# A two-layer attention and expert kernel: layer one's weighted values, one block of 32 products in every unit, become one block of 64 in every second unit

## The chip, the cores and the metric

The kernel runs on one core of a Trainium2 chip, all of it in one launch. The metric is the device time of that launch in microseconds; a lower one is better. TensorE (PE) multiplies, VectorE (DVE), ScalarE (ACT) and GpSimd (POOL) do the element-wise work, SyncE (SP) issues most DMAs. Each engine works through its own list of instructions in order and waits on semaphores that others raise.

## What is computed

Input: x (64 batches, 128 rows, 128 features), a side input of the same shape and a context of 120 rows per batch. In short:

```python
x = x + L0_xattn(layernorm(x), side, ctx, ctx)   # 16 heads of 8; keys: 128 projected + 120 given
x = x + L0_ffn(layernorm(x))                     # top 2 of 8 experts, silu(a) * g
x = x + L1_xattn(layernorm(x), ctx, ctx)         # 16 heads of 8; 120 keys
x = x + L1_ffn(layernorm(x))                     # top 2 of 8 adapters, gelu
# an attention, per batch and head:
attn = softmax(q @ k.T * scale); out = attn @ v
```

The change lies in the first line, the attention over 248 keys.

## The kernel before

`encoder` (L2066) runs five phases one behind the other: constants, layer one's attention (`attention_layer`, L103, with `first` true), the expert tiles, layer two's attention, the adapters. The 64 batches are 16 groups of four. A **step** g of the attention (L97) has eight **units** u; a unit is one batch and eight of its 16 heads. Step g scores group g, takes the row maxima of group g+1 and prepares g+2 and g+3. So steps 0 to 14 hold scores and maxima, step -1 maxima alone and step 15 scores alone.

Five engines walk the same list `UNIT` (L145). Its entries: **scores** i (L1033) is four bf16 products of 122 rows by 128 columns into one of three PSUM banks, i even for the 128 projected keys, i odd for the 120 others; ACT turns each into weights (`exponent`, L719, instruction L725) in `p_t`. **max** i (L1048) is two bf16 products of 248 columns into one of two banks (NMX = 2), and DVE reduces each to two columns of maxima (`row_maxima`, L873, instruction L876). **job** i is projections, transposes and router work at fixed places (table at L133); PE fills a misc bank (L978), ACT or DVE empties it. **values** i (L1066) is half of a unit's weighted values: with the two passes of an f32 product 16 of the 32 products of L1086, which work in four strips of PSUM `ps_o` side by side. It works on the unit before (`prev_unit`, L289), whose weights are complete by then.

What sets the order: PE, DVE and ACT each follow `UNIT` entry by entry; DVE and ACT have nothing at a values entry. DVE adds side work behind each maximum (`between`, L918: input statistics and the router's stages, table at L1445) and empties the jobs VP, OB and OP before the next maximum.

The waits that matter: PE's maximum tile n waits until DVE has read tile n-2 (L1059), its scores tile n until ACT has read n-3 (L1040). A values block waits for the weights of its unit (L1077), and in the first and fifth unit for ACT's copy of `ps_o` (L1080). ACT's weights buffers are two, so the first exponent of unit u waits until the values of unit u-2 are done (L724).

```python
wait(pe, max_read, i - NMX + 1)                                    # L1059
pe.wait_ge(sc_read, sc_no(g, u, (quarter + 1) * NT))               # L1077
wait(pv_done, g.n * UPS + u - 1)                                   # L724, on ACT, for i == 0
```

Of the kernel before, what the change touches and what calls it, by code (L numbers as in the profile page):

```python
# [81 lines left out]
def wait(eng, sem, value):  # L82

    if isinstance(value, int) and value <= 0:
        return
    eng.wait_ge(sem, value)
# [16 lines left out]
def attention_layer(nc, x_in, x_out, side_t_in, ctx_in, ctx_t_in, layer, consts, route, stacks, second, expert_w=None,  # L103
# [12 lines left out]
    first = layer == 0  # L116
# [26 lines left out]

    if first:
        UNIT = [  # L145
            ("job", 0), ("scores", 0), ("max", 0), ("scores", 1), ("job", 1), ("max", 1), ("values", 0),
            ("values", 1), ("scores", 2), ("max", 2), ("scores", 3), ("job", 2), ("max", 3),]
    else:
        UNIT = [
            ("job", 0), ("scores", 0), ("max", 0), ("scores", 1), ("values", 0), ("values", 1), ("job", 1),  # L150
            ("max", 1),]
# [5 lines left out]

    def stored_in(b):
        return -3 if b < 4 else -2

    def job_group(u, place, name, b):
        if name in ("SK", "SV"):
            return b - stored_in(b)
        if name == "XT" and not first:
            return 3
        if name == "KP" and not first:
            return 3
        if name in ("XT", "QP", "KP"):
            return 2
        if name == "VP":  # L170
            return 1 if first else 0
        if name == "RC":
            return -2
        if name in HEAD_JOBS:
            return 0
        if name in ("AT", "OP", "RX", "RQ"):
            return -1
        if name == "OB":
            return -1 if u < 3 else 0
        return 1 if u >= 2 else 0  # L180
    def head_step(name, b):
        return Group(0, 0) + (NG if (name, b) == ("FG", 1) else NG - 1)
    def job_runs(g, job):
        if job[2] in HEAD_JOBS:
            return g.n == head_step(*job[2:]).n
        if job[2] in ("SK", "SV"):
            return g.n == stored_in(job[3])
        if not first and job[2] in ("KP", "VP") and 0 < (g + job_group(*job)).n + (job[2] == "VP") <= STORED - (job[2] == "KP"):
            return False
        return (g + job_group(*job)).exists  # L190
# [21 lines left out]
    with ExitStack() as c:  # L212
# [76 lines left out]
        def prev_unit(g, u):  # L289
            return (g, u - 1) if u else (g + -1, UPS - 1)  # L290

        def jobs_at(g, u, place, engines_jobs=None):
            return [(k, j) for k, j in enumerate(jobs) if j[:2] == (u, place) and job_runs(g, j)
                    and (engines_jobs is None or j[2] in engines_jobs)]
# [4 lines left out]
        def stored_values(g):  # L299
            return not first and 0 <= g.n < STORED  # L300

        def emptied(eng, gj, name, b=0):

            n = job_done(gj, name, b) - 1
            if n >= 0:
                eng.wait_ge(misc_emptied[n % 2], n // 2 + 1)
# [668 lines left out]
        def _(pe):  # L975
# [57 lines left out]
            def scores(g, u, i):  # L1033

                b, hf, p = u // 2, u % 2, g.par
                t, quarter = CHUNKS[i]
                n = sc_no(g, u, i)
                if i == 0 and hf == 0 and b % 2 == 0:
                    pe.wait_ge(shift_loaded[p][b // 2], (g.pair + 1) * 32)
                wait(pe, sc_read, n - NSC + 1)  # L1040
                k0 = sum(KEYS[:t])
                for j in range(4):
                    h = hf * HALF + quarter * 4 + j
                    last = mm(ps_sc[n % NSC][0:KEYS[t], j * S:(j + 1) * S], k_st[p][:, b // 2, h, b % 2, k0:k0 + KEYS[t]],  # L1044
                              q_st[p][:, b // 2, h, b % 2], start=True, stop=True)
                last.then_inc(sc_filled, 1)

            def max_tile(g, b, k):  # L1048

                p = g.par  # L1050
                i = mx_no(g, b, k)
                if first and g.n == 0 and b == 0:
                    if k == 0:
                        pe.wait_ge(first_half_loaded, 16 * 2 * NPART)
                    elif k == MT_PER_B // 2:
                        pe.wait_ge(st_loaded[0][0], 16 * 2 * NPART)
                elif k == 0 and b % 2 == 0:
                    pe.wait_ge(st_loaded[p][b // 2], (g.pair + 1) * 16 * 2 * NPART)
                wait(pe, max_read, i - NMX + 1)  # L1059
                for j in range(HPB):  # L1060
                    h = k * HPB + j
                    last = mm(ps_mx[i % NMX][:, j * NK:(j + 1) * NK], q_st[p][0:TERM_TOP, b // 2, h, b % 2],  # L1062
                              k_st[p][0:TERM_TOP, b // 2, h, b % 2], start=True, stop=True)
                last.then_inc(max_filled, 1)

            def weighted_values(g, u, quarter):  # L1066

                b, hf, p = u // 2, u % 2, g.par
                if u == 0 and quarter == 0:

                    if stored_values(g):
                        pe.wait_ge(v_formed, g.n + 1)
                    else:
                        emptied(pe, g, "VP")
                    if first:
                        pe.wait_ge(v_ctx_ready, g.n + 1)
                pe.wait_ge(sc_read, sc_no(g, u, (quarter + 1) * NT))  # L1077
                if u % 4 == 0 and quarter == 0:

                    pe.wait_ge(o_read, g.n * 2 + b // 2 + 1)  # L1080
                for t in range(NT):
                    for strip in range(4):
                        j = quarter * 4 + strip
                        r, col = 32 * strip, ((b % 2) * 2 + hf) * S
                        at = (hf * 4 + strip) * V_PAIR + quarter * 2 * (DH + 1)
                        last = mm(ps_o[r:r + 2 * (DH + 1), col:col + S], v_t[t][p][:, b, at:at + 2 * (DH + 1)],  # L1086
                                  p_t[t][u % 2][:, j * S:(j + 1) * S], start=(t == 0 and quarter == 0),
                                  stop=(t == NT - 1 and quarter == 1))
                if quarter == 1:
                    last.then_inc(pv_done, 1)  # L1090

            def step(g):
                g1 = g + 1
                for u in range(UPS):
                    gp, up = prev_unit(g, u)
                    for what, i in UNIT:
                        if what == "job":
                            for k, j in jobs_at(g, u, i):
                                fill(g, k, j)
                        elif what == "scores" and g.exists:  # L1100
                            scores(g, u, i)
                        elif what == "max" and g1.exists:
                            max_tile(g1, u // 2, (u % 2) * MT_PER_U + i)
                        elif what == "values" and gp.exists:
                            weighted_values(gp, up, i)
            if first:
                pe.wait_ge(route.consts_loaded, 48)
            run_steps(pe, step, LAST_STEP)


# [955 lines left out]
def encoder(nc, a, out):  # L2066

    x3 = nc.dram_tensor("x3", (NG, S, GB, D), F32, kind="Internal").ap()
    xs = nc.dram_tensor("routed_in", (ROUTED_ROWS, ROW), F32, kind="Internal").ap()
    ys = nc.dram_tensor("routed_out", (TOKENS * TOP + 2 * E * S, D), F32, kind="Internal").ap()  # L2070
    x1, second = (ys[0:TOKENS * TOP].rearrange("(g k s b) d -> k g s b d", k=TOP, s=S, b=GB)[k] for k in range(TOP))
    with ExitStack() as c:
        route, stacks = Route(nc, c, xs), Stacks(nc, c)
        consts = constants(nc, c, a["w_attn"], a["b_attn"], a["b_rows"], a["wqkv_t"], route)
        attention_layer(nc, a["x"], x1, a["side_t"], a["ctx"], a["ctx_t"], 0, consts[0], route, stacks, second,
                        expert_w=(a["w1_t"], a["w2_t"]))
        expert_tiles(nc, ys, route, stacks)
        head = AdapterHead(nc, c, route, x3, a["wg_t"], a["bg"], a["W1_t"], a["W2_t"])
        attention_layer(nc, x1, x3, None, None, a["ctx_t"], 1, consts[1], route, stacks, second, head=head)
        adapter_layer(nc, x3, out, head)  # L2080
# [46 lines left out]
```

## Time and profile before

| | us |
|---|---|
| median of three runs | 1431.8 (1426.97 to 1435.11) |
| the profiled execution | 1426.79, its span 1424.7 |
| PE busy over the span | 1271.9 (89%) |
| DVE busy | 1072.4 (75%) |
| ACT busy | 838.4 (59%) |
| POOL busy | 882.7 (62%) |
| mean granted clock of TensorE | 0.952 |

Busy time of PE is the time in which at least one matmul is in the array; matmuls overlap, so an always busy PE can still have waits between them. The start-to-start distance in the timeline tells more. Layer one's blocks of values run from 72 to about 575 us of the span.

### The profile page before, as it was taken

Reading aid. Unit: us, or ns where it says so; the run is one execution under the profiler, and the core shown is the slowest. Engines: PE = TensorE matmul, PEld = TensorE weight load, DVE = VectorE, ACT = ScalarE, POOL = GpSimd, SP = SyncE. Lnnn points to the kernel's source line nnn. Section 1 sums busy time; section 2 is a strip of 40 time slices with the busy share of each in tenths; the row PEclk is TensorE's granted clock in tenths of the full one; section 3 lists DMA queues with packets and bytes.
Section 4 is the critical chain, followed back from the end, with each engine's and each line's share of the span. In section 5 each row is a group of like instructions: output and inputs, shape, how many; then the busy total and the mean of one; then the engine's idle time right before and its main releaser. Section 6 shows DMA issues by size and latency. Waiting matters only on the chain. (4 is left out here: it accounts for less than half of the span.)

```text
span 1424.7 us, 44434 instructions
## 1 busy us (share of the span) xinstructions
PE 1271.9 (89%) x16309; PEld 1054.9 (74%) x16309; DVE 1072.4 (75%) x3393; ACT 838.4 (59%) x1590; POOL 882.7 (62%) x949
## 2 busy tenths in 40 slices
PE   2689999999999999379999999668999999968998
PEld 0377787787777787279999999536777788746776
DVE  4678999989989996547766666457888888835774
ACT  3167777777777767156666666235666666634552
POOL 6346888888878856547777777534554444125660
PEclk9799999999999999689999999779999999968999
DMA  6776677777777760535555555487888888534784
GB/s 185 218 218 205 220 248 245 238 242 241 239 230 233 223 189 31 192 56 64 66 65 66 64 65 64 95 235 222 259 266 268 259 263 243 158 80 115 185 186 139
DMA packets 212638, 252.15 MB, mean 177 GB/s; under 512 B 38328, under 2 KB 173752, under 8 KB 205400
## 3 DMA queue, kind: packets, MB, share of 16 engines
q1 hardware_dynamic: 179768, 226.33, 52.7%
q0 software_dynamic: 25840, 21.71, 10.9%
q8 instruction: 131, 2.15, 0.6%
q10 hardware_dynamic: 6816, 1.29, 0.5%
q14 instruction: 83, 0.68, 0.2%
HBM read 156.73 MB, written 91.46 MB: 174 GB/s over the span
## 5 line engine op out<-in xcount | busy, mean ns | idle before, releaser
L876 DVE TENSOR_REDUCE L_neg_max<-L_ps_mx 128x2 f32<-128x496 f32 (+1 forms) x768 | 489.4, 661 | 100.9 <-PE L_ps_mx L1062 98.5
L725 ACT ACTIVATE L_p<-L_ps_sc 120x512 f32<-120x512 f32 (+1 forms) x768 | 417.5, 598 | 207.3 <-PE L_ps_sc L1044 203.7
L1062 PE MATMUL L_ps_mx<-stack_k,stack_q 118*128 118x248 bf16 (+1 forms) x2048 | 299.1, 250 | 42.7 <-DMA stack_q<-L_q_rows 26.1
L1044 PE MATMUL L_ps_sc<-stack_q,stack_k 122*120 122x128 bf16 (+1 forms) x3072 | 300.2, 221 | 3.7 <-ACT L_p L725 2.5
L1044 PEld LDWEIGHTS L_ps_sc<-stack_q,stack_k 122*120 122x120 bf16 (+1 forms) x3072 | 239.5, 123 | 56.8 <-issue 35.4
L1563 POOL DMA_INDIRECT routed_out<-M_y,M_x x135 | 212.0, 1570 | 87.8 <-DVE M_y L1654 86.8
L1086 PE MATMUL L_ps_o<-L_p,L_v 120*18 120x128 f32 (+1 forms) x6144 | 220.8, 276 | 2.5 <-ACT L_o_sb L754 2.1
L1062 PEld LDWEIGHTS L_ps_mx<-stack_k,stack_q 118*128 118x128 bf16 x2048 | 141.7, 100 | 103.4 <-issue 35.1
L1086 PEld LDWEIGHTS L_ps_o<-L_p,L_v 120*18 120x18 f32 (+1 forms) x6144 | 147.7, 98 | 37.7 <-issue 24.7
L1433 POOL DMA_INDIRECT routed_in<-R_xn,R_slot x128 | 127.0, 993 | 42.2 <-issue 36.2
L1609 ACT COPY M_w<-stack_k 128x768 f32 x135 | 112.1, 832 | 53.6 <-PE M_ps_g L1586 36.3
L1586 PE MATMUL M_ps_a<-M_xT,M_w 128*128 128x128 f32 x810 | 113.4, 276 | 0.0
L1586 PE MATMUL M_ps_g<-M_xT,M_w 128*128 128x128 f32 x810 | 113.2, 276 | 0.0
L1595 PE MATMUL M_ps_y<-M_w,M_hT 128*128 128x128 f32 x810 | 112.6, 275 | 0.0
L522 POOL TENSOR_TENSOR L_rem<-L_qf,L_q_parts_sb 128x512 f32<-128x512 f32 x30 | 34.8, 1161 | 122.0 <-ACT L_q_parts_sb L663 122.0
L1614 ACT ACTIVATE M_act_a<-M_ps_a 128x384 f32<-128x384 f32 x135 | 66.3, 491 | 73.0 <-PE M_ps_a L1586 72.4
L1586 PEld LDWEIGHTS M_ps_a<-M_xT,M_w 128*128 128x128 f32 x810 | 102.0, 193 | 0.1
L1586 PEld LDWEIGHTS M_ps_g<-M_xT,M_w 128*128 128x128 f32 x810 | 101.9, 193 | 0.0
L1595 PEld LDWEIGHTS M_ps_y<-M_w,M_hT 128*128 128x128 f32 x810 | 101.3, 192 | 0.2 <-DVE M_hT L1646 0.2
L1635 DVE COPY M_w<-stack_q 128x384 f32 x135 | 49.1, 364 | 63.4 <-issue 61.0
L1646 DVE TENSOR_TENSOR M_hT<-M_act_a,M_ps_g 128x384 f32<-128x384 f32 x135 | 74.8, 554 | 26.8 <-ACT M_act_a L1614 22.6
L522 POOL TENSOR_TENSOR L_rem<-L_kf,L_k_parts_sb 128x512 f32<-128x512 f32 (+1 forms) x23 | 27.8, 1209 | 72.1 <-ACT L_k_parts_sb L668 60.1
(211 smaller groups left out, 2150.3 us busy)
## 6 DMA issues: line engine op xcount, KB each, us to landing
L_q_rows<-L_q_parts_sb SPq DMA_DIRECT2D x192, 192.0 KB, 4.1
stack_q<-L_q_rows SPq DMA_DIRECT2D x189, 192.0 KB
stack_k<-L_k_rows SPq DMA_DIRECT2D x93, 372.0 KB
stack_k<-L_k_rows SPq DMA_DIRECT2D x96, 180.0 KB
F_spread<-F_gate_rows SPq DMA_DIRECT2D x32, 512.0 KB, 7.1
L_k_rows<-L_k_parts_sb SPq DMA_DIRECT2D x32, 372.0 KB, 4.3
M_x<-routed_in SPq DMA_DIRECT2D x135, 66.0 KB, 2.0
L_k_rows<-L_k_parts_sb SPq DMA_DIRECT2D x32, 180.0 KB, 4.3
```

Of the source, the lines that this page charges most:

```text
L725: nc.scalar.activation(p_t[t][u % 2][:, quarter * 4 * S:(quarter + 1) * 4 * S], ps_sc[n % NSC][0:KEYS[t], :], ACT.Exp).then_inc(sc_read, 1)
L876: nc.vector.tensor_reduce(neg_max[:, b, kk * HPB:(kk + 1) * HPB], v, AX.X, ALU.max, negate=True).then_inc(max_read, 1)
L1044: last = mm(ps_sc[n % NSC][0:KEYS[t], j * S:(j + 1) * S], k_st[p][:, b // 2, h, b % 2, k0:k0 + KEYS[t]], q_st[p][:, b // 2, h, b % 2], sta ...
L1062: last = mm(ps_mx[i % NMX][:, j * NK:(j + 1) * NK], q_st[p][0:TERM_TOP, b // 2, h, b % 2], k_st[p][0:TERM_TOP, b // 2, h, b % 2], start=Tr ...
L1086: last = mm(ps_o[r:r + 2 * (DH + 1), col:col + S], v_t[t][p][:, b, at:at + 2 * (DH + 1)], p_t[t][u % 2][:, j * S:(j + 1) * S], start=(t == ...
L1433: self.nc.gpsimd.indirect_dma_start(out=self.route.xs, out_offset=bass.IndirectOffsetOnAxis(ap=self.slot[g.par][:, b, k:k + 1], axis=0), i ...
L1563: nc.gpsimd.indirect_dma_start(out=ys, out_offset=bass.IndirectOffsetOnAxis(ap=token_row, axis=0), in_=y_t[ts % NY][:], in_offset=None, co ...
L1586: last = nc.tensor.matmul(out[:, k * S:(k + 1) * S], w1[th % NW][:, half + k * 128:half + (k + 1) * 128], xT[p][:], start=True, stop=True)
L1595: last = nc.tensor.matmul(ps_y[p][:, 0:D], hT[p][:, k * S:(k + 1) * S], w2[ty % NW][:, k * D:(k + 1) * D], start=(k == 0), stop=(k == FC - 1))
L1609: nc.scalar.copy(w1[tw % NW][:], w1_all[:, bass.ds(e_w * W1, W1)]).then_inc(w1_ready, 1)
L1614: nc.scalar.activation(act_a[p][:], ps_a[p][:, 0:FC * S], ACT.Silu).then_inc(silu_ready, 1)
L1646: nc.vector.tensor_tensor(hT[p][:], act_a[p][:], ps_g[p][:, 0:FC * S], ALU.mult).then_inc(hT_ready, 1)
```

## The change

In layer one both values entries move to a single place, behind the second scores and before job 1 and the second maximum. In odd units PE skips it. In even units it does the two halves of unit up-1, then the two halves of unit up, where up is the unit before. The number of products, what they read and write, all waits and the order on DVE, ACT, POOL and SP are as before. Layer two keeps its list.

```diff
     if first:
         UNIT = [
-            ("job", 0), ("scores", 0), ("max", 0), ("scores", 1), ("job", 1), ("max", 1), ("values", 0),
-            ("values", 1), ("scores", 2), ("max", 2), ("scores", 3), ("job", 2), ("max", 3),]
+            ("job", 0), ("scores", 0), ("max", 0), ("scores", 1), ("values", 0), ("job", 1), ("max", 1),
+            ("scores", 2), ("max", 2), ("scores", 3), ("job", 2), ("max", 3),]
...
+    PAIRED_VALUES = first
...
                         elif what == "max" and g1.exists:
                             max_tile(g1, u // 2, (u % 2) * MT_PER_U + i)
+                        elif what == "values" and PAIRED_VALUES:
+                            if u % 2 == 0 and i == 0 and gp.exists:
+                                for quarter in range(2):
+                                    weighted_values(gp, up - 1, quarter)
+                                for quarter in range(2):
+                                    weighted_values(gp, up, quarter)
                         elif what == "values" and gp.exists:
                             weighted_values(gp, up, i)
```

## Rows read from the trace of the kernel before

**Rows 1.** Busy time by stretch: us, PE, PEld, DVE, ACT, POOL, clock, DMA.
```profile
80.00:100.00 20.00, 17.73 (x321) 14.00 (x309) 16.00 (x31) 12.56 (x25) 7.04 (x8) 1.00 0.89 268
200.00:500.00 300.00, 291.69 (x4747) 236.17 (x4750) 274.81 (x903) 218.09 (x447) 254.50 (x286) 1.00 0.74 234
...
580.00:620.00 40.00, 9.64 (x73) 8.77 (x74) 16.47 (x88) 7.58 (x15) 16.84 (x18) 0.52 0.34 118
```
**Rows 2.** Waits, 200 to 500 us: who for whom, us in total, times, longest.
```profile
DVE L_neg_max L876 <- PE L_ps_mx L1062: 20.5, 42, 1.0
PEld L_ps_sc L1044 <- issue: 17.4, 77, 0.3
PEld L_ps_o L1086 <- issue: 13.9, 68, 0.2
```
**Rows 3.** Timeline of PE around one block of values: start us, length us.
```profile
304.77 0.39 PE L1044 MATMUL L_ps_sc<-stack_q,stack_k 122*120 122x128 bf16 x4
304.99 0.38 PE L1062 MATMUL L_ps_mx<-stack_k,stack_q 118*128 118x248 bf16 x2
305.30 1.07 PE L1086 MATMUL L_ps_o<-L_p,L_v 128*18 128x128 f32 x32
306.30 0.40 PE L1044 MATMUL L_ps_sc<-stack_q,stack_k 122*128 122x128 bf16 x4
```
**Rows 4.** Timeline, one maximum from PE to DVE and the bank back.
```profile
321.90 0.38 PE L1062 MATMUL L_ps_mx<-stack_k,stack_q 118*128 118x248 bf16 x2
...
322.31 1.26 DVE L876 TENSOR_REDUCE L_neg_max<-L_ps_mx 128x2 f32<-128x496 f32 x2 [0.24 <-PE L_ps_mx L1062]
...
323.13 0.37 PE L1062 MATMUL L_ps_mx<-stack_k,stack_q 118*128 118x248 bf16 x2 [0.20 <-issue]
```
**Rows 5.** DVE alone in four stretches of one group: us, busy (instructions), clock.
```profile
324.72:329.99 5.27, 5.25 (x19) 1.00 0.73 226
301.03:306.95 5.92, 5.24 (x22) 1.00 0.31 91
310.67:315.06 4.39, 4.36 (x18) 1.00 0.98 284
317.09:322.31 5.22, 3.85 (x7) 1.00 0.93 291
```
**Rows 6.** Timeline, the jobs that lie between the block's place and the second maximum.
```profile
299.82 0.63 PE L1014 MATMUL L_misc<-C_ident,L_att 128*128 128x128 f32 x4 [0.25 <-DVE L_att L811]
300.31 0.39 PE L1062 MATMUL L_ps_mx<-stack_k,stack_q 118*128 118x248 bf16 x2
...
308.20 1.11 PE L1003 MATMUL L_misc<-C_w,L_srcT 128*128 128x128 f32 x8
...
310.00 0.75 DVE L795 TENSOR_TENSOR L_v<-L_misc,C_bias_bc 128x256 f32<-128x256 f32 x2
310.67 0.67 DVE L876 TENSOR_REDUCE L_neg_max<-L_ps_mx 128x2 f32<-128x496 f32 x1
...
316.23 0.61 PE L1401 MATMUL L_misc<-C_ident,R_xn 128*128 128x128 f32 x4
316.68 0.38 PE L1062 MATMUL L_ps_mx<-stack_k,stack_q 118*128 118x248 bf16 x2
```
**Rows 7.** Timeline, router products: filled by PE, taken by DVE.
```profile
318.88 0.97 PE L1405 MATMUL L_misc<-C_wT,R_xnT 128*128 128x24 f32 x8
...
320.16 0.42 DVE L1269 TENSOR_TENSOR R_products<-R_qkv 128x256 f32<-128x256 f32 x1 [0.26 <-ACT R_qkv L1384]
```
**Rows 8.** Timeline of PE, first block of unit 1 of steps 0, 2, 9, 13, 15.
```profile
72.28 1.07 PE L1086 MATMUL L_ps_o<-L_p,L_v 128*18 128x128 f32 x32
...
136.00 1.07 PE L1086 MATMUL L_ps_o<-L_p,L_v 128*18 128x128 f32 x32
...
359.96 1.07 PE L1086 MATMUL L_ps_o<-L_p,L_v 128*18 128x128 f32 x32
...
490.59 1.07 PE L1086 MATMUL L_ps_o<-L_p,L_v 128*18 128x128 f32 x32
...
552.00 1.07 PE L1086 MATMUL L_ps_o<-L_p,L_v 128*18 128x128 f32 x32 [0.77 <-ACT L_o_sb L754]
```
**Rows 9.** Timeline of ACT: two exponents behind each other.
```profile
306.74 1.09 ACT L725 ACTIVATE L_p<-L_ps_sc 128x512 f32<-128x512 f32 x2 [0.90 <-PE L_ps_sc L1044]
```

## The prediction

> **What bounds the kernel now.** I read the busy time by stretch first. In layer one PE is busy 292 of 300 us at the full clock and DVE 275 of 300 [rows 1]: two engines near their end, with 25 us of idle on DVE and little on PE. The waits come next. DVE's idle is nearly all waiting for PE's maxima, 20.5 us. On PE the largest groups are issue gaps of 0.2 us ahead of the values' weight loads and behind them, 68 and 77 times in some 74 units [rows 2]. The timeline shows what they are: from a maximum to the next scores PE needs 0.22 us start to start, from a maximum to a block of values 0.31, an entry cost of 0.09. The block is 1.07 long, less 0.27 for its last product 0.80, and the next scores start 0.20 after the start of the last product, while one set of four strips takes 0.80/7 = 0.115; so leaving costs 0.09 [rows 3]. One group takes 223.96/7 = 31.99 us from step 2 to step 9 [rows 8]. PE sets the pace and DVE follows at 92%.
>
> **What the change removes.** Of 128 blocks 64 go, so 64 entries and exits: 64 x 0.18 = 11.5 us of PE, 0.72 us per group. If PE alone counted, that would be the whole result.
>
> **What it moves.** DVE can only be two maxima behind PE, since there are two banks. Before, 1.0 us of values stood in each unit between the second and the third maximum. Now about 2.0 us stand between the first and the second of every even unit, and the seven others of the pair follow with no values between them, faster than DVE can reduce them. The wait that decides runs in a circle: first maximum of the even unit on PE, the long block, second maximum, its reduction, DVE's work in order up to the third maximum of the odd unit, and only then PE may write the first maximum of the next even unit. The length of this circle is a floor under a pair of units. Its terms:
>
> - First maximum to second, start to start: the maximum 0.22, scores 0.22, entry 0.09, sixteen sets of strips at 0.115 = 1.84, exit 0.09, in all 2.46 [rows 3].
> - Second maximum to its reduction on DVE: 322.31 - 321.90 = 0.41 [rows 4].
> - DVE from that reduction to the one of the third maximum of the odd unit: five reductions and the side work between them. The four stretches of one group show it with DVE's idle left out: 5.25, 5.24, 4.36 and 3.85, in all 18.70. I take 18.4, since two reductions behind each other stand 1.26 - 0.67 = 0.59 apart, so work that is packed hides about 0.08 of each tail that stood free in these rows [rows 4, 5].
> - From the start of that last reduction until PE may write: 323.13 - 322.31 = 0.82 [rows 4].
> - The jobs at place 1 of even units now stand in the circle: the transposes at 299.82 take 0.49, the router's at 316.23 take 0.45. The value projection costs more. PE fills it from 308.20, about 0.95; DVE starts to empty it some 1.15 after the first product's start (0.84 to the last start, 0.31 until it can be read) and needs 0.67 before the reduction. Against a reduction 0.41 behind the block that is 1.15 + 0.67 - 0.41 = 1.41 [rows 6].
> - In the fourth pair the router's first products are ready 320.16 - 318.88 = 1.28 after PE starts to fill them [rows 7]. The fill follows the fourth maximum, which waits for the second's reduction (0.82), so it starts 1.04 behind that reduction and DVE has its data at 2.32; three reductions end at 1.76. A wait of 0.56.
>
> A group of four pairs: 4 x (2.46 + 0.41 + 0.82) + 18.4 + 0.49 + 0.45 + 1.41 + 0.56 = 36.07 us, against 31.99 and against PE's own 31.99 - 0.72 = 31.27. So DVE's circle is the bound, and a group becomes 4.08 us longer. In words: DVE's idle per pair grows, because a block of 2 us outlasts the at most two maxima it holds.
>
> **The other steps.** Steps 2 to 12, eleven groups, took 490.59 - 136.00 = 354.6 us before, with three groups a little long; 11 x 36.07 = 396.8 gives +42. Steps 0 and 1 took 63.7. They lack the router's stages of two groups behind (weighing, logits, picks, slots: my estimate is 3 us, somewhat under half of the 18.4 - 20 x 0.59 = 6.6 us of side work in the circle): 72.1 - 6 = 66, +2. Steps 13 and 14 took 61.4; they lack the input statistics, about 1.1 each: 69.9, +8.5. Step 15 has no maxima, so PE's saving stays there: 4 x 0.18, -0.7 [rows 8]. Sum +52 us. What lies ahead of step 0 and behind step 15 is untouched.
>
> **Edits that cost nothing.** ACT's first exponent of an even unit now waits for the first half of the block, through its weights buffer: that half is done 0.22 + 0.22 + 0.09 + 0.80 + 0.27 + 0.04 = 1.64 after the first maximum's start, where ACT used to start about 0.2 after it. ACT is late by 1.4 us in each even unit. Cover: eight exponents at 1.09 - 0.60 = 0.49 are 3.9 of a pair's 9 us [rows 9], and ACT is busy 218 of 300 [rows 1]. Queued behind are jobs that DVE takes; the closest is the exponential of the router's products in unit 0, which I put at 3.1 where DVE comes for it at 3.45. If that cover of 0.3 goes, the circle grows (second rival). PE's wait for the weights of unit u-1 is easier met than before in the first half, and the last quarter comes 1.5 us later than PE now asks. Its wait for the copy of ps_o falls a unit later. POOL and the DMAs get more time per group; the order of SP and POOL does not change.
>
> **The sum.** The profiled execution took 1426.8: 1426.8 + 52 = 1479. It stands 5.0 under the median of the runs shown; from the median the forecast is 1431.8 + 52 = 1484. About 0.5%, 7 us, is what a measurement of this kernel can tell from no change.
>
> **The rivals.**
>
> *PE's saving comes through.* The 64 exits and entries go and DVE keeps pace: 1431.8 - 11.5 = 1420. For it: PE has the higher busy share, and the gaps are there to be read [rows 2]. Against it: a maximum needs 0.59 on DVE and 0.44 with its scores on PE, so a block twice as long must leave DVE idle unless it held 2.4 us of work, and it may hold two tiles. It would decide only if DVE's side work fell mostly behind the block; 6.6 us of it lie in the circle. The Trainium skill, TensorEngine Tiling (Array Packing), Key Properties, says that a change of tiling mode drains the engine; by that rule alone fewer blocks are a gain, and the 0.18 per block agrees with it. Chance 0.05. That the two effects about cancel, with DVE's side work covering most of the longer block: 0.05, at 1432.
>
> *ACT's late start joins the circle.* Place: the exponential of the router's products, which DVE's stage behind the second maximum of unit 0 waits for; or any job that ACT empties late. Price: up to 1.4 us in one pair of four, 15 x 1.4 = 21, 1505; it decides from the point where ACT is more than 0.3 later than reckoned. Chance 0.06.
>
> *The clock.* PE would be busy with some 31.3 of 36 us, 87%, in gaps under 1 us. It kept the full clock from 80 to 100 us at 17.7 of 20 busy, and had 0.52 where it was busy a quarter of the time [rows 1]. At the half clock a group would need 2 x 31.3 = 62.6 in place of 36; if a tenth of layer one went so, that is 1.6 groups x 26.6 = 42 us, 1526. The Trainium skill, TensorE: Matmul & The Clock Gate, Part 1, says that idle stretches of PE halve its clock; by that the change would be worse than forecast, and no gap here is as long as those where the trace shows it. Chance 0.03.
>
> **How the numbers follow.** The circle 0.81, its own range from +38 (if packed side work is 0.5 us shorter per group and the first and last steps gain nothing) to +66 (18.7 and some 0.7 us of further waits per group): 1470 to 1498. PE's saving 0.05, no change 0.05, ACT 0.06, clock 0.03. The range for eight in ten goes 1465 to 1502. Faster by over 0.5% 0.05, within 0.5% 0.05, slower 0.90. If it is not slower, the first rival has it: less waiting on PE and DVE at the same pace.
>
> **What would show it.** In the profile after, a steady group should take 36 us, with blocks x64 and 2.0 us from start to the next work. DVE should wait for PE's maxima once per pair, about 1 to 2 us, some 5 to 6 us per group against 20.5/9.4 = 2.2 now; PE should wait for DVE ahead of maxima, where now it hardly does. The gaps around values should halve in number. ACT's first exponent in even units should be released by PE's values. If a group stays near 32 us, the circle is wrong; if ACT's router exponential is what DVE waits for, the second rival is at work; a clock under 1.0 between 80 and 550 us would mean the third. Expert tiles, layer two and the adapters should take what they did.

## The result and the profile after

The changed kernel takes 1475.0 us (median of four runs, 1472.2 to 1476.4), the kernel before beside it 1430.8. The ratio is 1.030, with an interval of 1.026 to 1.033. The profiled execution took 1476.35 with a span of 1474.6, 49.9 us over the span of before.

Where the 49.9 us lie, by the starts of the first maximum of each step: up to the end of step 1 5.0, in steps 2 to 12 37.3 (391.9 against 354.6), in step 13 3.1, in step 14 3.2, behind the last maximum 1.2. Before step -1 and behind the last product of values nothing changed by more than 0.2.

The page of the profile, DVE's reduction and PE's maxima, both layers together (busy, mean ns of one, idle ahead of them and who ended it). Before:

```profile
L876 DVE TENSOR_REDUCE L_neg_max<-L_ps_mx 128x2 f32<-128x496 f32 (+1 forms) x768 | 489.4, 661 | 100.9 <-PE L_ps_mx L1062 98.5
...
L1062 PE MATMUL L_ps_mx<-stack_k,stack_q 118*128 118x248 bf16 (+1 forms) x2048 | 299.1, 250 | 42.7 <-DMA stack_q<-L_q_rows 26.1
```

After:

```profile
L878 DVE TENSOR_REDUCE L_neg_max<-L_ps_mx 128x2 f32<-128x496 f32 (+1 forms) x768 | 485.3, 658 | 133.7 <-PE L_ps_mx L1064 132.3
...
L1064 PE MATMUL L_ps_mx<-stack_k,stack_q 118*128 118x248 bf16 (+1 forms) x2048 | 301.2, 252 | 91.0 <-DVE L_neg_max L878 58.9
```

Both engines wait more than before, each mostly for the other. The busy time by stretch says the same of the steady part; it answers to [rows 1]:

```profile
200.00:500.00 300.00, 268.20 (x4327) 224.18 (x4315) 245.88 (x803) 201.93 (x408) 230.16 (x258) 1.00 0.69 215
```

PE falls from 292 to 268 us in 300, DVE from 275 to 246; the clock stays full. Now the waits of the same stretch, against [rows 2]:

```profile
ACT L_p L727 <- PE L_ps_o L1088: 60.1, 34, 2.8
PEld L_ps_mx L1064 <- DVE L_neg_max L878: 41.7, 83, 1.0
DVE L_neg_max L878 <- PE L_ps_mx L1064: 39.3, 26, 2.2
...
DVE L_v L797 <- PE L_misc L1005: 9.8, 8, 1.2
```

DVE waits 39.3 us in 26 long waits where it had 20.5 in 42 short ones, and 9.8 for the value projection, which it never waited for before: together 5.8 us per group, where the prediction said 5 to 6. PE's maxima wait for DVE 83 times, before 18 times.

One pair of units on PE, the fourth, with the block and the second maximum:

```profile
305.99 0.39 PE L1064 MATMUL L_ps_mx<-stack_k,stack_q 118*128 118x248 bf16 x2 [0.32 <-DVE L_neg_max L878]
306.21 0.39 PE L1046 MATMUL L_ps_sc<-stack_q,stack_k 122*120 122x128 bf16 x4
306.53 1.96 PE L1088 MATMUL L_ps_o<-L_p,L_v 128*18 128x128 f32 x64
308.42 0.66 PE L1409 MATMUL L_misc<-C_ident,R_xn 128*128 128x128 f32 x4
308.92 0.38 PE L1064 MATMUL L_ps_mx<-stack_k,stack_q 118*128 118x248 bf16 x2
```

and on DVE beside it:

```profile
305.27 1.82 DVE L878 TENSOR_REDUCE L_neg_max<-L_ps_mx 128x2 f32<-128x496 f32 x3
309.33 0.67 DVE L878 TENSOR_REDUCE L_neg_max<-L_ps_mx 128x2 f32<-128x496 f32 x1 [2.24 <-PE L_ps_mx L1064]
```

The reader sees the whole story in these seven lines. The first maximum waits for DVE, because both banks are full. The block runs from 306.53 to 308.42. DVE has its two maxima reduced by 307.1 and then stands idle for 2.24 us, until the second maximum comes.

The block of 64 costs PE 308.42 - 306.21 - 0.22 = 1.99 us. Two blocks of 32 cost 2 x (0.31 + 1.00 - 0.22) = 2.18 [rows 3], so the pairing does save 0.19 us of PE's time per pair, as reckoned; it just does not matter.

### The profile page after: what moved, and what is told of

It is laid out like the page before. It is cut to its first block and busy times, and to the rows that moved or that the text cites. A ratio compares the mean times of both kernels' runs of the same rounds, so it can differ in the third digit from the quotient of the medians.

```text
span 1474.6 us, 44434 instructions
## 1 busy us (share of the span) xinstructions
PE 1280.7 (87%) x16309; PEld 1076.5 (73%) x16309; DVE 1065.5 (72%) x3393; ACT 844.1 (57%) x1590; POOL 886.3 (60%) x949
## 5 line engine op out<-in xcount | busy, mean ns | idle before, releaser
L1046 PEld LDWEIGHTS L_ps_sc<-stack_q,stack_k 122*120 122x120 bf16 (+1 forms) x3072 | 250.2, 123 | 37.4 <-ACT L_p L727 12.4
L1064 PEld LDWEIGHTS L_ps_mx<-stack_k,stack_q 118*128 118x128 bf16 x2048 | 137.8, 100 | 173.2 <-DVE L_neg_max L878 92.6
L1088 PE MATMUL L_ps_o<-L_p,L_v 120*18 120x128 f32 (+1 forms) x6144 | 210.0, 277 | 0.8 <-ACT L_o_sb L756 0.7
L1088 PEld LDWEIGHTS L_ps_o<-L_p,L_v 120*18 120x18 f32 (+1 forms) x6144 | 154.2, 98 | 15.5 <-issue 1.2
```

## The experiments

The measure that tells most is the time of a pair of units, from the start of the first maximum of the even unit to that of the next even unit, as the median of steps 2 to 11. These figures are worked out from the start times in each trace; the group is the sum of the four medians. The ratio is to the kernel before on the same chip. Four runs on a chip where the kernel before took 1555 us are told in the first section below and are not in the table.

| kernel | (0,1) | (2,3) | (4,5) | (6,7) | group | ratio, interval |
|---|---|---|---|---|---|---|
| before | 7.81 | 8.81 | 8.02 | 7.35 | 31.99 | |
| changed | 8.74 | 9.20 | 9.45 | 8.21 | 35.60 | 1.030 (1.026 to 1.033) |
| place alone | 7.87 | 8.91 | 9.48 | 8.13 | 34.39 | 1.021 (1.015 to 1.027) |
| pairing alone | 8.76 | 9.67 | 8.78 | 8.10 | 35.31 | 1.028 (1.023 to 1.034) |
| job 1 ahead of the pair | 8.78 | 9.64 | 8.91 | 8.18 | 35.51 | 1.031 (1.026 to 1.037) |
| changed, three banks for maxima | 9.35 | 8.44 | 8.54 | 7.30 | 33.63 | 1.014 (1.009 to 1.020) |
| before, three banks for maxima | 7.88 | 8.65 | 7.94 | 7.35 | 31.82 | 1.002 (0.998 to 1.005) |
| changed, exponents later still | 9.37 | 9.30 | 9.52 | 8.32 | 36.51 | 1.040 (1.034 to 1.045) |
| short maxima, single blocks | 8.77 | 8.76 | 7.73 | 7.01 | 32.27 | 1.000 (0.997 to 1.003) |
| short maxima, pairing alone | 8.98 | 8.40 | 8.00 | 7.11 | 32.49 | 1.002 (0.999 to 1.005) |

### Place alone, and three more, on a disturbed chip

```diff
-            ("job", 0), ("scores", 0), ("max", 0), ("scores", 1), ("job", 1), ("max", 1), ("values", 0),
-            ("values", 1), ("scores", 2), ("max", 2), ("scores", 3), ("job", 2), ("max", 3),]
+            ("job", 0), ("scores", 0), ("max", 0), ("scores", 1), ("values", 0), ("values", 1), ("job", 1),
+            ("max", 1), ("scores", 2), ("max", 2), ("scores", 3), ("job", 2), ("max", 3),]
```

> The kernel before with its block of 32 moved to the changed kernel's place (behind scores 1, ahead of job 1 and maximum 1), in every unit. It parts the place from the pairing. If the long block and the run of seven maxima behind it are the cause, the place alone costs little: the circle per unit is 0.44 + 1.10 + 0.41 + 0.59 + 0.82 = 3.36, eight of them 26.9, with the jobs 2.35 and the side work behind each second maximum about 2.5 some 31.8, no more than PE's own time: a group of 31.8 to 33.0 us, 1429 to 1447 in all. If the place is the cause (the jobs and the value projection now standing between block and maximum), a group stays near the changed kernel's 35.6 and the time near 1475.

On the chip that ran this and the next three, the kernel before took 1555.2 us in place of 1430.8, so totals from there say little. The ratio was 1.007 (1.004 to 1.010). The loss of that chip in this kernel is in one place: the fourth pair took 15.3 us, where the same kernel takes 8.13 on the undisturbed chip. One line of the timeline shows its kind, PE idle in the middle of its list and released by nothing that the profile shows ("issue"):

```profile
334.62 0.39 PE L1062 MATMUL L_ps_mx<-stack_k,stack_q 118*128 118x248 bf16 x2 [3.73 <-issue]
```

The second and third pair stood at 8.91 and 9.47 in the median, within 0.01 us of what the undisturbed chip gives below. The expectation failed: it averaged the circle over the group, found it no longer than PE's own time, and missed that the circle must be closed unit by unit. In unit 4 alone it is 0.44 + 1.10 (block) + 1.41 (value projection) + 0.41 + 0.59 + 0.82 = 4.77 (measured 4.84), and unit 5, where a job with transposes stands in the same gap, makes up the rest of the 9.47 (4.63).

Two of the three others replaced the row maxima by shorter ones, first with single blocks, then as in the changed kernel:

```diff
                 v = ps_mx[mx_no(g1, b, kk) % NMX][:, 0:HPB * NK].rearrange("q (h s) -> q h s", h=HPB)
+                if first:
+                    v = v[:, :, 0:NK // 2]
```

> The kernel before, layer one's row maxima taken over the first half of the columns of each head alone (124 of 248; the maxima of the second half are left out), so that a reduction takes DVE about 0.33 in place of 0.59. DVE has slack; PE is then alone the bound. Expected: the stalls of PE ahead of maxima, 9 us in 300, go, a group of about 31.0 us, some 1415 in all. It is the base for the next run.

> The changed kernel with the same halved row maxima. The circle shrinks by 24 reductions x 0.26 = 6.2 us to about 29.4, under PE's time. If DVE's circle is the cause, the pairing now pays what it saves on PE: a group 0.7 us shorter than in the run with single blocks and halved maxima, about 30.3, and 8 to 13 us less in all (ratio about 0.992). If something else makes the pairing slow (ACT's late start, a wait of PE on weights, the long block itself), it stays slower than the single blocks here too, by tens of us.

They gave 1549.6 and 1570.3 us (ratios 0.997 and 1.009). The base did not get as fast as expected: its two clear pairs took 8.77 and 7.74 against 8.81 and 8.02 before, where some 1 us less per group was expected of all four. In the two clear pairs the changed order stood at 8.64 and 8.44 against 8.77 and 7.74: 0.13 less in the one, 0.70 more in the third pair, where the value projection now stands in the gap. The expected gain did not come, and the expectation had said that this would speak for another cause than DVE. But place and pairing were mixed in it, and two of the four pairs were disturbed, so it decides nothing; the last section asks again.

The fourth parted the two blocks of the pair by job 1 and the second maximum:

```diff
-            ("job", 0), ("scores", 0), ("max", 0), ("scores", 1), ("values", 0), ("job", 1), ("max", 1),
+            ("job", 0), ("scores", 0), ("max", 0), ("scores", 1), ("values", 0), ("job", 1), ("max", 1), ("values", 1),
...
-                            if u % 2 == 0 and i == 0 and gp.exists:
...
+                            if u % 2 == 0 and gp.exists:
+                                for quarter in range(2):
+                                    weighted_values(gp, up - 1 + i, quarter)
```

> The changed kernel with the pair of blocks in even units parted by job 1 and maximum 1: unit up-1 at its place, unit up behind maximum 1. As many entries and exits as before the change, but all values still in even units. Bunching theory: the circle is 0.44 + 1.10 + 1.54 + 0.41 + 4 x 0.585 + 0.82 = 6.65 per pair against 6.6 of the changed kernel, less the side work behind maximum 1 and a part of the value projection: a group of about 35, 1465 in all. Rival, that it is the single long block that starves DVE: with a maximum in its middle the group falls to 32 to 33, about 1440.

It took 1595.1 us in a single execution, with a disturbed fourth pair of 16.6 us. The clear pairs, the second and the third, were 9.38 and 9.05, against 9.20 and 9.45 in the changed kernel and 8.81 and 8.02 before. The formula in the expectation, with the jobs and the side work as this trace has them, gives 6.65 + 0.49 + 2.25 = 9.39 and 6.65 + 0.95 + 1.50 = 9.10. So a maximum in the middle of the long block does not bring the pairs back to those of before: what counts is all that PE does between the first maximum and the run of six that DVE must then work off. As far as two pairs show it, the rival of the one long block is out.

### Place alone again, on an undisturbed chip

The edit is the first one of the section above: single blocks of 32 in every unit, at the changed kernel's place.

> [...] By the pairs that stood clear in the first look (7.9, 8.91, 9.47, fourth unknown, 7.35 to 7.8) a group should take 33.6 to 34.1: some 1455 to 1462 in all. That would put over half of the change's loss on the place and the rest on the pairing. If the place matters little, 1431 to 1440.

1459.6 us, ratio 1.021, a group of 34.39. So the place by itself, with no pairing at all, loses 2.4 us per group, nearly all in the third and fourth pair. The third is told by these lines of its timeline, of PE and then of DVE:

```profile
324.97 0.37 PE L1062 MATMUL L_ps_mx<-stack_k,stack_q 118*128 118x248 bf16 x2
325.18 0.39 PE L1044 MATMUL L_ps_sc<-stack_q,stack_k 122*120 122x128 bf16 x4
325.50 1.07 PE L1086 MATMUL L_ps_o<-L_p,L_v 128*18 128x128 f32 x32
326.50 1.16 PE L1003 MATMUL L_misc<-C_w,L_srcT 128*128 128x128 f32 x8
```

```profile
327.70 0.76 DVE L795 TENSOR_TENSOR L_v<-L_misc,C_bias_bc 128x256 f32<-128x256 f32 x2 [0.58 <-PE L_misc L1003]
328.37 1.24 DVE L876 TENSOR_REDUCE L_neg_max<-L_ps_mx 128x2 f32<-128x496 f32 x2
```

PE starts the first maximum at 324.97, and DVE reduces the second at 328.37. In between, when DVE has reduced the first, two small operations are all that it can do; then it waits 0.58 for the projection and needs 0.67 to empty it, which it used to do while values ran.

### Pairing alone, at the old place

```diff
-            ("job", 0), ("scores", 0), ("max", 0), ("scores", 1), ("values", 0), ("job", 1), ("max", 1),
+            ("job", 0), ("scores", 0), ("max", 0), ("scores", 1), ("job", 1), ("max", 1), ("values", 0),
             ("scores", 2), ("max", 2), ("scores", 3), ("job", 2), ("max", 3),]
```

> The changed kernel with its block of 64 back at the place of the kernel before, behind job 1 and maximum 1, in even units: pairing alone. Circle from the second maximum of the even unit: 2.46 + 0.41 + 5 x 0.585 + 0.82 = 6.61 and the side work from the third maximum of the even unit to the fourth of the odd one: pairs about 9.5, 9.15, 8.05 and 7.9 us, a group of 34.6 (changed kernel 35.6). The value projection then costs nothing. If the place alone made the change slow, the pairs fall to those of before (7.8, 8.8, 8.0, 7.35).

1468.6 us, ratio 1.028, a group of 35.31. Measured as the expectation did, from second maximum to second maximum, the pairs are 9.70, 9.62, 8.29 and 7.70 against 9.5, 9.15, 8.05 and 7.9. The pairing alone loses 3.3 us per group. Together place and pairing lose 3.6, not 5.7: both lengthen the same circle. Once the maxima are bunched, the place adds 0.67 in the third pair and gives back 0.47 in the second.

Not all of the 3.3 is DVE's distance to PE. In the first pair DVE waits for an exponential of ACT, whose work starts late in every even unit:

```profile
310.45 0.42 DVE L1292 TENSOR_REDUCE R_sum<-R_exps 128x32 f32<-128x256 f32 x1 [1.18 <-ACT R_exps L1397]
```

Behind this wait DVE reduces the third maximum 0.84 us after PE has started it, where in the other pairs it is 0.41 or 0.42. So about 0.4 us of the 3.3 is the second rival, ACT's late start, at this place of the block.

Nor does the value projection cost nothing here, as the expectation had it. The second pair came 0.5 longer than the sum, and its end shows why:

```profile
325.46 0.37 PE L1064 MATMUL L_ps_mx<-stack_k,stack_q 118*128 118x248 bf16 x2
...
325.89 1.11 PE L1005 MATMUL L_misc<-C_w,L_srcT 128*128 128x128 f32 x8
326.84 0.38 PE L1064 MATMUL L_ps_mx<-stack_k,stack_q 118*128 118x248 bf16 x2
```

```profile
325.63 0.65 DVE L878 TENSOR_REDUCE L_neg_max<-L_ps_mx 128x2 f32<-128x496 f32 x1
```

The second maximum starts at 326.84, 1.21 us behind the reduction that frees its bank. In the first pair 0.72 is enough for that. Here the projection stands in front of it on PE.

Another wait looks worse than it is. PE's transposes of the attention output wait for DVE, as they did before the change, but now ahead of the block:

```profile
PEld L_misc L1016 <- DVE L_att L813: 4.0, 9, 0.5
PE L_misc L1016 <- DVE L_att L813: 3.1, 9, 0.3
```

The maximum behind them starts at 317.22, and 316.50 + 0.72, the reduction that frees its bank and the way back, is the same moment: here the wait costs next to nothing.

### Job 1 ahead of the pair

```diff
-            ("job", 0), ("scores", 0), ("max", 0), ("scores", 1), ("values", 0), ("job", 1), ("max", 1),
+            ("job", 0), ("scores", 0), ("max", 0), ("scores", 1), ("job", 1), ("values", 0), ("max", 1),
```

> The changed kernel with job 1 ahead of the block of 64 and maximum 1 behind it. All jobs still stand in the circle on PE, but DVE empties the value projection during the block. Circle theory: only the third pair gets shorter, by 0.46 (0.67 of emptying less the 0.21 that the maximum takes anyhow), 8.99 in place of 9.45, others 8.74, 9.20, 8.21; group 35.1. Rival (the jobs' place has no part in it): nothing moves.

The third pair came to 8.91 (expected 8.99, changed kernel 9.45): the value projection's share of the loss is about what it was reckoned at. The second pair grew by 0.44 to 9.64, which was not expected. The wait of the transposes for DVE, whose two lines stand word for word in this trace too, now lies between the first and the second maximum: from one to the other PE takes 3.39 us in place of 2.91. So the total did not move (1475.0).

### Three banks for the maxima

```diff
-        NSC, NMX = 3, 2
+        NSC, NMX = (2, 3) if first else (3, 2)
```

> The changed kernel with three PSUM banks for maxima and two for scores in layer one. PE may now be three maxima ahead, so one reduction and the side work behind the second maximum of the odd unit leave the circle. From the changed kernel's pairs (8.74, 9.20, 9.45, 8.21 us) that makes 7.87, 8.15 to 8.25 (PE's own time there), 8.58, 7.29: a group of 32.0 where the chip is undisturbed, if the score banks cost nothing; with their cost 32 to 34. If DVE's distance to PE is not what makes the pairs long, they stay at 8.74, 9.20, 9.45, 8.21 or grow by the lost score bank.

> The kernel before with the same three and two banks. It prices the lost score bank and asks for a kernel that beats both. PE's stalls ahead of maxima (about 1 us in a group) go; a score bank comes back about 1.16 after its scores start, PE wants it after 0.87, so up to 0.3 per two scores tiles comes where PE isn't held up otherwise. Expected: a group between 31.3 and 33.5, pairs 7.8, 8.8, 8.0, 7.3 moved by no more than 0.4 each, ratio to before 0.985 to 1.03.

With single blocks the exchange of a bank moves nothing (1432.2 us, ratio 1.002). With the pair it takes the group from 35.60 to 33.63 and the time to 1449.7: the second, third and fourth pair come to 8.44, 8.54 and 7.30 (expected 8.15 to 8.25, 8.58, 7.29). That one more bank helps the paired order and not the other shows that the distance between PE and DVE is what the pairing runs out of. The first pair got longer, 9.35 where 7.87 was expected. There the scores, now with two banks, wait for ACT. From 200 to 500 us such waits of the weight loads add up to 24.3 us, against 3.9 in the changed kernel, and the longest stand in this pair:

```profile
340.38 0.23 PEld L1046 LDWEIGHTS L_ps_sc<-stack_q,stack_k 122*128 122x128 bf16 x4 [1.24 <-ACT L_p L727]
340.39 0.40 PE L1046 MATMUL L_ps_sc<-stack_q,stack_k 122*128 122x128 bf16 x4 [0.97 <-ACT L_p L727]
```

A smaller part lies ahead of the second maximum, which comes 2.74 us after the first in place of 2.42; why was not tried.

### ACT later still

```diff
-                    wait(act, pv_done, g.n * UPS + u - 1)
+                    wait(act, pv_done, g.n * UPS + u - (u % 2 if first else 1))
```

> The changed kernel with ACT's first exponent of an even unit held back until the whole block of 64 is done (it now waits for its first half): ACT starts 0.9 us later still, on PE and DVE nothing changes. If ACT's late start has no part in the loss, the pairs stay at 8.74, 9.20, 9.45, 8.21 but for the first, where DVE needs ACT's exponential with only 0.3 to spare: up to 0.6 there, 0 to 10 us in all. If ACT's start is in the circle, each pair grows by about 0.9 and the whole by some 55 us.

1486.6 us, 11.6 over the changed kernel. The first pair grew by 0.63, the others by 0.07 to 0.11. Were ACT's start in the circle, each would have grown by 0.9. In the changed kernel itself the spare time in the first pair can be read off: the exponential ends at 316.91 + 0.42 = 317.33 and DVE takes it at 317.64.

```profile
316.91 0.42 ACT L1397 ACTIVATE R_exps<-R_products 128x256 f32<-128x256 f32 x1
...
317.64 0.41 DVE L1292 TENSOR_REDUCE R_sum<-R_exps 128x32 f32<-128x256 f32 x1
```

With ACT later this wait appears in every group:

```profile
DVE R_sum L1292 <- ACT R_exps L1397: 4.3, 8, 0.5
```

Step 15, which has no maxima, is another matter: from the last maximum to the last product of values PE takes 25.60 us before, 25.79 with the place alone, 26.75 in the changed kernel and 29.34 here. There ACT's start does set the time.

### Pairing with DVE out of the way

```diff
+                if first:
+                    v = v[:, :, 0:NK // 8]
```

The second of the two runs also has the list of "Pairing alone, at the old place".

> The kernel before, layer one's row maxima taken over the first 31 of each head's 248 columns alone (the rest is left out of the maxima), so that DVE is far from its end. PE alone should be the bound: pairs at or a little under those of before (7.81, 8.81, 8.02, 7.35), group 31.0 to 31.6, ratio to before about 0.99. Base for the next run.

> The same short row maxima, with the pair of blocks at the old place in every second unit: pairing alone, with DVE out of the way. If DVE is what makes the pairing slow, the saving on PE now shows: 4 x 0.18 = 0.7 us per group under the run with single blocks, some 8 to 12 us in all, ratio between the two about 0.993. If ACT's late start, PE's waits for weights or the block itself are at work, it stays equal or slower.

1428.9 and 1433.8 us, groups of 32.27 and 32.49. The pairing's loss of 3.3 us per group shrinks to 0.2 as soon as DVE's reductions are short, so nearly all of that loss needs DVE's long reductions. The totals, 4.9 us apart, can hardly be told from each other: single executions of either kernel spread over 12 to 15 us. But the gain of 0.7 did not come, and the base did not get faster either. Two other waits stand right behind. In the base, PE's key projection in the first pair waits for its input (some 1 us per group), and so that pair is 8.77:

```profile
PE L_misc L999 <- DMA L_srcT<-in_side_t: 8.2, 8, 1.9
```

With the pair, DVE and PE wait for ACT, which starts late in every even unit:

```profile
DVE R_sum L1294 <- ACT R_exps L1399: 20.5, 8, 3.2
PEld L_ps_sc L1048 <- ACT L_p L727: 14.4, 40, 1.2
```

That is the rival of ACT's late start, hidden in the steady part of the changed kernel. That it takes the gain here is read from these waits; no run removes them.

## Why the prediction was right, point by point

The forecast was 1484 with a range of 1465 to 1502; 1475.0 lies in it. By the profiled executions it was +52, measured +49.9. By the medians the change is +44.2, since the profiled execution of before happened to lie 4 us under its median and that of after 1.4 over; that, not the mechanism, is most of the distance of 9 us.

**The removed switches.** 0.18 us per pair forecast, 0.19 measured, without effect on the time in steps with maxima, as forecast.

**The circle.** Forecast 36.07 us per group, measured 35.60. Term by term in one group after: from first maximum to the reduction of the second 2.84, 3.32, 4.28 and 3.34 (forecast 2.87, 3.36, 4.28, 3.32). From there to the reduction of the third maximum of the odd unit 5.16, 5.07, 4.45 and 4.07, together 18.75 (forecast 18.4 + 0.56). From that reduction until PE writes again 0.75, 0.80, 0.72 and 0.81 (forecast 0.82 each). The sum is 35.61. Two terms were taken too long, by 0.2 each: the return, and DVE's stretch, where the wait in the fourth pair was 0.48 and not 0.56 and the packed side work a little shorter than 18.4. The fourth pair shows the circle closed:

```profile
313.40 0.66 DVE L878 TENSOR_REDUCE L_neg_max<-L_ps_mx 128x2 f32<-128x496 f32 x1
```

```profile
314.21 0.27 PE L1064 MATMUL L_ps_mx<-stack_k,stack_q 118*128 118x248 bf16 x1 [0.38 <-DVE L_neg_max L878]
```

**The words for it.** "A block of 2 us outlasts the at most two maxima it holds" is half of the story. Place alone loses 2.4 of the 3.6 us with blocks of 1 us, through the jobs that moved into the gap. The sum had these as terms (1.41 for the value projection is what the trace shows), but the text laid the loss on the pairing. The runs show that either half of the change does most of the damage alone. And in the run with the pairing alone 0.4 us per group came from ACT, so "DVE's circle" there is not DVE and the two banks alone.

**The other steps.** Steps 2 to 12 +37.3 (forecast +42), steps 0 and 1 +4.6 (forecast +2), steps 13 and 14 +6.3 (forecast +8.5). Step 15 was wrong in sign: -0.7 forecast, +1.2 measured behind the last maximum. Without maxima DVE plays no part, and ACT's late start, which the forecast covered with the long pair, has no cover there: the run that delays ACT further lengthens this step by another 2.6 us. The waits from 597 us on:

```profile
ACT L_p L727 <- PE L_ps_o L1088: 4.5, 4, 1.3
PEld L_ps_sc L1046 <- ACT L_p L727: 3.4, 9, 0.9
```

**The rivals.** PE's saving did not come through, and the runs with short maxima say that it would not have with a faster DVE either. ACT's start was outside the circle by 0.3 us, as reckoned, and decides in step 15. From 71 us to the end of step 15 the clock fell once, at the start of step 1, to half for 7 us, while PE waited 2.6 us for the query stack's load. Before the change PE waited 1.5 us at that place, and the clock stayed full. In the steady part it stayed full in both. The stretch of the fall:

```profile
98.00:105.00 7.00, 5.91 (x80) 4.57 (x81) 1.35 (x2) 1.44 (x3) 0.00 (x0) 0.51 0.83 251
```

The first block of 64 of step 1 lies in this stretch and took 3.62 us in place of 1.96:

```profile
100.04 3.62 PE L1088 MATMUL L_ps_o<-L_p,L_v 128*18 128x128 f32 x64
```

Step 1 took 37.1 us against 35.6 in the steady part; in the run with the exponents later still, whose clock did not fall there, it took no more than a steady step, 36.5. So the fall may be worth about 1.5 of the +4.6, which is an estimate from these two traces. The rest of the distance to +2 stays open; the 3 us per step for the router's missing stages was an estimate that no run tested.

None of the complete kernels run beats the kernel before; the nearest, with three banks for the maxima, cannot be told from it. (Those with short maxima leave a part of the work out.)

## What to carry to other kernels

Where an engine fills two banks and another empties them, work out the longest circle through both, for each part of the period by itself: all that the first engine does between two fills counts in full, and how much it does elsewhere is no comfort. Saving time on the busier engine by gathering its long operations is worth nothing once the other engine runs dry during them; and a job moved into that gap costs its own time and the time to empty it. Look at what stands right behind the first bound before counting a gain: here a DMA and a third engine took the gain as soon as DVE's reductions were short.

## What was not expected of the hardware

Entering and leaving the blocks that work in four strips cost 0.09 us each at both lengths that were run: 1.99 us for 64 products against 2.18 for two of 32. And the chips used differ: on one, the same kernel took 1555 us in place of 1431, with a mean granted clock of 0.91 in place of 0.95. The trace of the place alone from there shows PE, DVE and ACT standing for 3.7 to 5.0 us, released by nothing that the profile can name, while GpSimd sent the router's rows with indirect DMAs. The second and third pair kept their median times to 0.01 us. GpSimd sends the same rows on the other chips without such a stop. What stops the engines there was not settled.
